# Gate stage with four ternary buffers and late down weights, and one shared down product moved to the end

## What is computed

```python
def bitlinear(x, w, norm_w):                 # gate/up: 1024 -> 2 x 2816, down: 2816 -> 1024
    xn = rms_norm(x, norm_w)
    xq = round(xn * 127 / max|xn|) per row   # integers in bf16
    wq = clip(round(w / mean|w|), -1, 1)     # ternary; one scale for the whole matrix
    return (xq @ wq.T) * scales
h = silu(gate) * up;  y = bitlinear(h, w_down, norm_down)
...
moe = sum over top-2 experts of weight * (silu(h@Wg) * (h@Wu)) @ Wd
sh  = silu(h@SWg) * (h@SWu) @ SWd            # shared expert, all tokens
x   = x + moe + sh
```

## Time and profile before

| | us |
|---|---|
| median of 3 runs | 701.76 (701.29 to 702.33) |
| the profiled execution | 699.4 |
| its span, first to last instruction | 697.6 |
| PE busy | 637.2 (91%) |
| DVE busy | 495.6 (71%) |
| ACT busy | 397.9 (57%) |
| POOL busy | 137.6 (20%) |
| mean granted PE clock | 0.983 |

### The profile page before, as it was taken

How to read it: one execution, slowest core, us unless ns; L and a number is a source line. 1 busy time by engine, 2 the same in 40 slices (tenths; PEclk the granted TensorE clock), 3 DMA queues, 4 the chain that set the end, 5 groups by cost and what they waited for, 6 DMA issues and landing times.

```text
span 697.6 us, 9765 instructions
## 1 busy us (share of the span) xinstructions
PE 637.2 (91%) x3276; PEld 476.2 (68%) x3289; DVE 495.6 (71%) x799; ACT 397.9 (57%) x524; POOL 137.6 (20%) x140
## 2 busy tenths in 40 slices
PE   4899999999998997769999999999999999999991
PEld 3778888877784342334567888787878778878771
DVE  5887778886787678888798429937465586473886
ACT  3788887887549576542673207717162673443750
POOL 2463444428401133411000400000000000000022
PEclk9999999999999999989999999999999999999996
DMA  9967776856988868606148516974738299292948
GB/s 344 371 239 307 288 287 242 333 210 220 402 343 350 344 220 337 278 0 224 49 178 305 232 70 248 363 292 168 313 132 349 95 385 390 70 382 91 352 140 321
DMA packets 30968, 179.00 MB, mean 257 GB/s; under 512 B 3808, under 2 KB 3808, under 8 KB 14688
## 3 DMA queue, kind: packets, MB, share of 16 engines
q1 hardware_dynamic: 25920, 161.39, 59.7%
q0 software_dynamic: 5024, 17.30, 6.5%
HBM read 155.62 MB, written 23.07 MB: 256 GB/s over the span
## 4 chain that ended last, share of the span: by engine, by line
PE 54%; ACT 16%; DVE 15%; issue 6%; DMA 5%; POOL 2%; DVEq 1%; ACTq 0%; POOLq 0%; SPq 0%
PE BK L288 10%; PE BK L282 10%; PE BK L283 10%; PE BK L276 6%; PE BK L1665 5%; DVE WL L945 4%; PE BK L1608 4%; ACT PR L1198 4%; ACT RA L1171 3%; ACT WH L1376 2%; PE BK L1757 2%; PE BK L1554 2%; PE BK L1539 1%; DVE HB L822 1%; DMA NG<-n_gate 1%
## 5 line engine op out<-in xcount | busy, mean ns | idle before, releaser
L282 PE MATMUL BK<-WH,ETH 128*128 128x512 f32 x272 | 107.5, 395 | 0.4
L283 PE MATMUL BK<-WL,ETH 128*128 128x512 f32 x272 | 106.0, 390 | 0.0
L945 DVE TENSOR_TENSOR WL<-RA,WH 128x2048 fp32r<-128x2048 f32 x40 | 89.1, 2286 | 9.1 <-ACT WH L1376 9.0
L1376 ACT ACTIVATE WH<-RA 128x2048 fp32r<-128x2048 f32 x40 | 73.5, 1922 | 3.1 <-PE BK L1665 3.1
L1608 PE MATMUL BK<-TG,XQ 128*128 128x512 bf16 x282 | 64.2, 386 | 11.9 <-DVE TG L796 10.2
L288 PE MATMUL BK<-WH,ETL 128*128 128x512 f32 x272 | 67.4, 390 | 0.0
L1429 ACT ACTIVATE HTH<-BK 128x256 fp32r<-128x256 f32 x34 | 12.1, 384 | 93.5 <-PE BK L1757 93.4
L282 PEld LDWEIGHTS BK<-WH,ETH 128*128 128x128 f32 x272 | 51.0, 188 | 15.9 <-DVE WL L945 4.2
L1608 PEld LDWEIGHTS BK<-TG,XQ 128*128 128x128 bf16 x288 | 28.1, 99 | 47.2 <-issue 8.9
L635 POOL DMA_INDIRECT GA<-rows,SLOT x4 | 4.7, 1176 | 277.5 <-SPq L525 276.6
L959 DVE TENSOR_TENSOR HE<-BK,SI 128x256 f32<-128x256 f32 x34 | 12.8, 420 | 64.5 <-PE BK L288 63.6
(11 more groups left out here) (245 smaller groups left out, 1368.9 us busy)
## 6 DMA issues: line engine op xcount, KB each, us to landing
RA<-wbit SPq DMA_DIRECT2D x51, 1024.0 KB, 6.4
RA<-wmoe SPq DMA_DIRECT2D x40, 1024.0 KB, 6.7
RC<-wmoe SPq DMA_DIRECT2D x20, 1024.0 KB, 7.5
RD<-wbit SPq DMA_DIRECT2D x9, 1024.0 KB, 7.8
rows<-ZERO POOLq DMA_DIRECT2D x34, 256.0 KB, 12.4
XG<-rows SPq DMA_DIRECT2D x15, 512.0 KB, 7.2
rows<-YS SPq DMA_DIRECT2D x14, 512.0 KB, 6.6
RA<-wqk SPq DMA_DIRECT2D x8, 640.0 KB, 7.4
```

Source lines behind the costliest of these rows:

```text
L282: e.matmul(dst, sh, mh, start=first and i == 0, stop=False)
L283: e.matmul(dst, sh, ml, start=False, stop=False)
L945: e.tensor_tensor(WL[m][:, q * RAW:q * RAW + RAW], RC[j][:, :], WH[m][:, q * RAW:q * RAW + RAW].bitcast(f32), ALU.subtract)\
L1376: e.activation(WH[m][:, q * RAW:q * RAW + RAW], RC[2 * m + q][:, :], ACT.Copy)\
```

## The change

- SP issues the down loads later: chunks 0 and 1 around the first gate loads, 2, 3, 8, 9, 10 spread over the later groups, 6, 7 and 4, 5 last, through the raw buffers RB[2], RB[3], RB[0], RB[1].
- The ternary weights of group c go to `gate_buffer(c)`: the two TG and the two TX in turn. DVE clamps group c+3 (not c+2) after group c.
- ACT rounds all down chunks and clamps 4 and 5 itself; DVE clamps the others. ACT's rounding of a group's two chunks stands between silus.
- The transposes and evacuation of tile 3's XQ stand earlier; PE waits for groups 2 and 3 block by block.
- The fifth and later blocks of TAIL use the SG buffers that are free; SGB goes.
- The zero writes are issued after POOL's last `norm_down`; DVE waits for them before the copy of HE.
- The down product of tiles 0 and 1 goes by thirds of k, in turn.
- Shared tile 2 keeps its transposed hidden rows (HTKH, HTKL, in H3's space) and returns before its down product; the split of expert 1's down weights comes first. In the last shared tile `kept_result` runs that product (banks 4, 5) between the up product and the transposes.
- The gathers' two halves get semaphores of their own; DVE adds routed rows of two tiles, the kept result, the routed rows of two more, and the last product's halves at the end.

```diff
 def tail_gate(c, t): return t - 2 if c == 10 and t >= 2 else t           # new
 def gate_buffer(c): return TG[c % 4] if c % 4 < 2 else TX[c % 4 - 2]     # new
 ...
# SP
-            down_load(0, 0, None)
             for n in range(4):
                 bit_load(n, 4 + n, "tern", 1 + n)
+            down_load(0, 0, None)
             ...
+            for n in range(4):
                 bit_load(n, 8 + n, "tern_a", 1 + n)
             e.wait_ge(s("zq"), NT)
             down_load(1, 1, None)
             for n in range(4):
                 bit_load(n, 12 + n, "tern", 5 + n)
-            for i in range(2, 6):
-                down_load(i, i % 2, i - 1)
...
+            for n in range(2):
+                bit_load(n, 16 + n, "tern", 9 + n)
+            down_load(2, 0, 1)
+            for n in range(2, 4):
+                bit_load(n, 16 + n, "tern", 9 + n)
+            down_load(3, 1, 2)
             for n in range(2):
                 bit_load(n, 20 + n, "tern", 13 + n)
+            down_load(8, 0, 3)
+            for n in range(2):
+                bit_load(2 + n, 2 * GC + 6 + n, "tern", 15 + n)
+            down_load(9, 1, 4)
+            for n in range(2):
+                bit_load(n, 2 * GC + 4 + n, "tern", 17 + n)
+            down_load(10, 0, 5)
# POOL, before and after the norm_down calls
-            for half in range(2 * (XT_TILES - NS)):
-                zero_rows(half)
...
+            e.memset(ZERO[:, :], 0.0).then_inc(s("zero_in"), 1)
+            e.wait_ge(s("zero_in"), 1)
+            for half in range(2 * (XT_TILES - NS)):
+                zero_rows(half)
# DVE
+            gate_weights(4)
+            group(2)
+            gate_weights(5)
+            pair_max(0)
+            group(3)
+            gate_weights(6)
+            group(4)
+            gate_weights(7)
+            down_clamp(0, RD16A)
+            pair_max(1)
...
+            group(7)
+            gate_weights(10)
+            down_clamp(3, RD16)
...
-            for t in range(1, NS):
+            for t in range(1, NS - 1):
                 shared_tile(t)
-                if t == NS - 1:
-                    split(1, 0)
-                    split(1, 1)
                 shared_result(t, t)
             split(1, 2)
+            split(1, 0, (0,))
+            e.wait_ge(s("rows"), 1)
+            hidden(NS - 1, HTKH, HTKL)
+            split(1, 0, (1,))
+            rows_lo(NS)
+            split(1, 1)
+            e.sem_inc(s("ys_d"), 1)
...
             split(NE + 1, 0)
+            result(total)
             split(NE + 1, 1)
-            result(total)
             split(NE + 1, 2)
             hidden(total)
...
+            routed(0)
+            routed(1)
+            shared_result(NS - 1, total, 4)
+            waits(e, ("ys_d", total + 2))
+            routed(NS - 1)
+            routed(NT - 1)
+            e.wait_ge(s("fin"), NT)
+            waits(e, ("y2_pe", total + 3))
             for q in range(2):
+                if q:
+                    e.wait_ge(s("sh_last"), 1)
+                v = XRES[:, NT - 1, q * 512:q * 512 + 512]
+                e.tensor_tensor(v, bank[2 + q], v, ALU.add).then_inc(s("fin"), 1)
# ACT
+            def group(c):
+                j, use = 2 * ((c + 3) % 2), (c + 3) // 2
+                gate_block(c, 0)
+                gate_block(c, 1)
+                rounded(j, use)
+                gate_block(c, 2)
+                gate_block(c, 3)
+                rounded(j + 1, use)
+            group(2)
+            group(3)
+            rounded_down(RD[:, :], s("raw_d"), 1)
+            group(4)
+            rounded_down(RD2[:, :], s("raw_e"), 1)
...
+            group(7)
+            rounded_down(RD[:, :], s("raw_d"), 3)
+            gate_block(8, 0)
+            gate_block(8, 1)
+            rounded_down(RD2[:, :], s("raw_e"), 3)
+            gate_block(8, 2)
+            gate_block(8, 3)
+            rounded_down(RB[0][:, :], in_b[0], 6)
             for n, (c, t) in enumerate(TAIL):
-                if n == 4:
-                    rounded_last(2)
-                    rounded_last(3)
...
+                if n == 1:
+                    rounded_down(RB[1][:, :], in_b[1], 6)
+                elif n == 3:
+                    sign_down(4, 0, 7)
+                elif n == 4:
+                    rounded_down(RB[2][:, :], in_b[2], 5)
+                elif n == 6:
+                    rounded_down(RB[3][:, :], in_b[3], 5)
...
+            hidden_t(0)
+            rounded_down(RD[:, :], s("raw_d"), 4)
+            sign_down(5, 1, 8)
+            hidden_t(1)
# PE
+            for c in (2, 3):
+                e.wait_ge(s("tern_a"), 2 * c - 2)
+                for t in range(NT):
+                    e.wait_ge(s("h"), 9 + HEAD.index((c - 2, t)))
+                    gate_block(gate_buffer(c), 4 * (c % 2) + t, t)
+            for c in range(4, 9):
+                gate_group(c, c % 2, gate_buffer(c), "tern", 2 * c - 2)
...
             hidden_t(0)
+            e.wait_ge(s("h"), 8 + 36 + 4)
+            e.wait_ge(s("ternd"), 4)
+            down_group(0, 0)
+            hidden_t(1)
+            e.wait_ge(s("h"), 8 + 44)
+            down_group(1, 0)
+            e.wait_ge(s("tern_a"), 6)
+            e.wait_ge(s("ternd"), 8)
+            down_group(0, 1)
+            down_group(1, 1)
...
+            def kept_result():
+                waits(e, (free_c[4], NE + 2), (free_c[5], NE + 2))
+                for q in range(2):
+                    for h in range(2):
+                        highs(e, bank[4 + q], y_high(h, q, HTKH), h == 0)
+                    m = lows(e, bank[4 + q], y_low(q, HTKL))
+                m.then_inc(s("y2_pe"), 1)
```

More of the change, by code:

```diff
@@ L1304, in _ @@
             sign(3, 3)
[L1305 removed]
             e.preload_act_table(ACT.Silu)
+            rows_out(3)
             def head_block(n):
@@ L1318, in head_block @@
                     .then_inc(s("silu"), 1)
-            for n in range(3):
-                head_block(n)
-            rows_out(3)
-            for n in range(3, 6):
+            for n in range(7):
                 head_block(n)
             rounded(0, 2)
+            head_block(7)
             rounded(1, 2)
-            for n in range(6, 8):
-                head_block(n)
-            rounded(2, 2)
-            rounded(3, 2)
-            rounded_down(0)
-            def gate_block(n, t, bank_):
-                waits(e, ("g_pe", n + 2), ("h", n + 5))
-                e.activation(SG[t][:, :], bank_[:, 0:GW], ACT.Silu, scale=col(9)[:, t:t + 1]).then_inc(s("silu"), 1)
@@ L1350, in _, with gate_block, group @@
-            for j in (0, 1):
-                rounded(j, 5)
-            gate_group(8, 0)
-            e.wait_ge(s("ternd"), 9)
+            def gate_block(c, t):
+                n = 4 * c + t
+                waits(e, ("g_pe", n + 2), ("h", n + 5))
+                e.activation(SG[t][:, :], bank[4 * (c % 2) + t][:, 0:GW], ACT.Silu, scale=col(9)[:, t:t + 1])\
+                    .then_inc(s("silu"), 1)
+            def group(c):
+                j, use = 2 * ((c + 3) % 2), (c + 3) // 2
[5 more added lines that the diff above has]
+                rounded(j + 1, use)
@@ L1438, in _ @@
             e.activation(WT[:, 1, :], E1[:, :, :].rearrange("p a b -> p (a b)"), ACT.Exp).then_inc(s("e1"), 1)
-            for t in range(1, NS):
+            for t in range(1, NS - 1):
                 hidden(t)
+            split(1, NS - 1, (2,))
+            e.wait_ge(s("rows"), 1)
+            hidden(NS - 1, True, HTKH)
             e.sem_inc(s("ys_a"), NS)
-            split(1, NS)
+            split(1, NS, (1,))
             e.wait_ge(s("ys_d"), NS)
@@ new lines, in _ @@
+            e.wait_ge(s("tern_a"), 6)
+            e.wait_ge(s("ternd"), 8)
+            down_group(0, 1)
+            down_group(1, 1)
+            e.wait_ge(s("ternd"), 9)
+            down_group(0, 2)
+            hidden_t(2)
+            down_group(1, 2)
+            for t in (2, 3):
+                e.wait_ge(s("hqt"), 3 * t + 3)
+                e.wait_ge(s("x3"), t - 1)
+                for q in range(2):
+                    down_part(t, q, 0, KB).then_inc(s("d_pe"), 1)
+                    if t == 2 and q == 0:
+                        hidden_t(3)
@@ L1758, in tile @@
                     m.then_inc(s("ht2_pe"), 1)
-                if more:
-                    rows_t(t + 1, 1, rows)
+                if not more:
+                    last_result(t)
+                    return
+                rows_t(t + 1, 1, rows)
+                if isinstance(t, int) and t == NS - 1:
+                    e.sem_inc(s("y2_pe"), 1)
+                    return
                 left = [("ys_a", t + 1), ("ys_d", t + 1)] if not isinstance(gi, int) or gi else [("ys_d", t)]
-                waits(e, ("ht_hi", t * 2 + 1), *left, (free_c[4], gi + 1), (free_c[5], gi + 1))
@@ L1773, in tile, with down_at, y_high @@
                 e.wait_ge(s("ht_lo"), t * 2 + 2)
                 for q in range(2):
```

(24 more changed lines are left out.)

244 lines of the change are left out of this document (102 added, 142 removed).

## The result

| | before | after |
|---|---|---|
| median, 4 runs each on one chip | 701.52 us (700.08 to 702.33) | 681.67 us (681.32 to 683.29) |
| the profiled execution | 699.4 | 681.58 |
| its span | 697.6 | 680.0 |
| mean granted PE clock | 0.983 | 0.987 |

Ratio 0.972, 95% interval 0.9699 to 0.9741: faster. Two more batches measured the changed kernel at 683.08 (0.9753) and 683.13 (0.9743), 5 runs each, so 682 to 683 is the fairer figure. The medians before and after are 19.9, 17.1 and 17.8 us apart in the three batches. Forecast: 681.5, range 676 to 691.

The account below looks back on a forecast made before the run. PE was taken as held up in the gate stage, mostly by late ternary weights, and the end as set by gathers and DVE. Terms -1.7 - 15.3 + 0.9 - 5.2 + 1.0 = -20.3 gave 681.5 us, range 676 to 691.

Parts of the forecast that it names:

- Zero rows: Before the gate stage: with the zero writes issued later, NG lands sooner and PE's wait at ZQ goes, -1.7 us.
- Gate stage: PE runs the gate blocks without waiting for ternary weights; the HQ transposes start near 296.0, not 311.25: -15.3 us.
- From there the queue never empties: Gate stage: after down 1's clamp at 250.3 the load queue stays full, so down 9 lands at 277.8.
- bounds 0 to +3: Gate stage: DVE clamps stretched beside POOL in five places, 0 to +3 us in all, taken as 0.
- Down product: Down product of the first tiles by thirds: PE waits for HQT, 46.6 us instead of 45.7, +0.9, bounds 0 and +3.8.
- Moved product: Third shared tile's down product moved to the end: tile 3's transposes come sooner, -5.2 us, bounds -5.4 and -2.
- End: After the up product: gathers land sooner but DVE starts later with a longer list, +1.0 us, bounds -3 and +3.
- A: Rival, gate stage: the loads, not ACT, set the pace; four laps pay 1.8 us each, 689 us; chance 0.17.
- B: Rival, gate stage: late raw weights hold silus, hidden blocks and the clamps that free buffers; slower, 704 us; chance 0.04.
- C: Rival, experts: the moved product brings nothing; the middle gives back 5 us, the end pays 1, 686.5 us; chance 0.08.
- D: Rival, gate stage: PE still waits for clamps, so only -9.5 us comes, 692 us; chance 0.06.

Follow-up runs that it names:

- the narrow products: The changed kernel with each of POOL's norm products in the gate stage covering 16 columns, the rest left out: 663.66 us, ratio 0.9478 to the kernel before.
- the clamps moved ahead: The changed kernel with DVE's clamps of down 1 and 3 in front of gate clamps 8 and 10: 681.12 us, ratio 0.9719 to the kernel before.
- the execution with both changes: The changed kernel with down clamps 1 and 3 ahead and the last tile's transposes before the kept result: 681.30 us, ratio 0.9723 to the kernel before.
- the six executions: Six profiled executions with the changed kernel's gate stage; first gate matmul to first HQ transposes took 88.7 us in the mean.
- the experiment: The changed gate stage with the experts and end of the kernel before, kept product undone: 686.93 us, ratio 0.9807 to the kernel before.
- the run with late clamps: The changed kernel with gate clamps 4 to 10 a group later, first three down clamps moving too: 714.70 us, ratio 1.0205 to the kernel before.

## Why the prediction was right, and where its steps were not

1. **Zero rows** (-1.7). First ZQ transposes at 184.82 without a wait, against 187.10: -2.3. DVE's weight scales came at 174.08 (forecast 174.5), NG in 4.0 us. The writes took longer to issue than in the earlier trace rows, and held nobody:

```profile
308.17 21.89 POOL L572 DMA_DIRECT2D rows<-ZERO  x34 [0.32 <-POOL ZERO L627]
```

2. **Gate stage** (-15.3). Transposes of HQ at 297.13, against 311.25: -14.1 with item 1 in it, -11.8 without. Short by 3.5. PE's part was right: no waits but 0.8, clock 1.00, through at 286 (288.1 less item 1 is 286.4). The step that failed is "From there the queue never empties". It stood on a down clamp that follows its gate clamps at once, and on a stretch of DVE's clamps beside POOL taken as 0 since "such a clamp delays a load whose queue is full anyway". The trace has the DMA share at 0.48 at that very clamp. ACT waited 6.7 us, not 3.9, and began down 9's rounding 71.1 us behind the first gate matmul, where the forecast had 277.8 - 210.6 = 67.2. That is 3.9 late and so the whole miss. The two stretches of 4 us at 135 and 320 GB/s are worth 2.7 and 1.0 us of a queue that moves 430, an estimate, and come to as much. The stretch of the clamps was in the earlier trace rows with bounds 0 to +3; the narrow products put it at 1.8, and the clamps moved ahead, which get round the same stretch, at 2.0 (1.3 in the execution with both changes). With the clamps ahead the same two stretches move 375 and 418 GB/s, and down 9's rounding still begins at 69.0; what holds back that rest was not tried. The Trainium skill (SBUF — State Buffer, "SBUF: two separate sides") has the port pair of DVE and GpSimd as an exclusive lock that the first takes for its whole instruction. The pair of clamps at 2.91 beside POOL and 1.30 without its long products agrees; I had used that rule for POOL's issues alone and not for DVE's clamps.
3. **Down product** (+0.9): 45.92 against 45.74: +0.2, and +0.6 in the mean of the six executions. PE's wait for HQT was there, 0.91. Within its bounds.
4. **Moved product** (-5.2): from tile 1's transposes to tile 3's 32.69 us against 437.36 - 399.62 = 37.74: -5.05; by the experiment -4.97. The lower clock that the new wait brought in two of twelve executions (+1.5) had no term. PE waited 1.41 for ETH and not again, 1.1 and 0.3 had been forecast.
5. **End** (+1.0): from the last up product to the last instruction +0.75, DVE without a gap, as told. The end of the kernel before took 21.95 and 23.01 us in the two executions that have it, so neither the size nor the sign of this term is shown.

The profiled spans differ by 17.6, the sum had 20.3: the gate stage's 3.5 too much, against it 0.6 that item 1 brought beyond its term and 0.7 that item 3 cost less, and small ones. That the median fell on the forecast is partly luck: the profiled execution before was 2.4 us quicker than its median, the one after was not, and that offset, added to the forecast, covered the miss. In the profiled execution's own terms the forecast was 679.1, and it took 681.58. Against the later batches (683.1) the forecast is 1.6 low.

Of the rivals, A's sign (loads late, by latency and issue) was in part true, at 3.5 us and not 7.5; B's ring exists and is dear, but half a group's delay does not close it and a whole group's, with the down clamps behind it, does; C and D fell, by the run without the kept product and by PE's 0.8 us of waits.

## What to carry to other kernels

- On an engine that works in order, what a late load costs is what stands behind its consumer. Putting that consumer behind the work that needs nothing from it brought 4.0 us here, twice what an earlier load did.
- A stage fed by a ring of buffers (clamp, issue, landing, rounding, clamp) has slack or it has none: half a group later cost 0.2 us, a group later with the down clamps behind it over 31. Work out a lap with the latency of one load before pricing a delay as a single step.
- The instruction that releases the next load goes in front of its neighbours, above all where these are stretched.
- A gain that ends in front of a dense stretch of PE is partly given back where PE enters that stretch sooner but at a low granted clock and ahead of its operands: of 5.3 us gained ahead of the down product, 2.6 went in it.

## What was not expected of the hardware

- DVE's int16 to bf16 clamps of 128x2048 take 0.65 us, and 1.3 to 1.45 in the mean of a pair beside POOL's 128x512 products; whichever kind of clamp comes first is hit (a down clamp moved to that place took 1.23 instead of 0.68).
- POOL's issues were slower beside DVE work with two operands in SBUF: 2.11 and 1.87 us for a gather beside the WL split, 0.93 behind it, and up to 1.72 when DVE's sums were moved beside them. The plain zero writes took 21.89 / 34 = 0.64 us each beside DVE's work in the down product, against 0.54. Only the sums were moved by an experiment; for the split and the zero writes the cause is argued from what ran beside them.
- A short wait of PE can cost as much again. In ten of the twelve profiled executions with the moved product the matmuls behind the wait for ETH took their usual 0.39 to 0.40 us, with the granted clock at 1.00; in two they took up to 0.63, with 0.57 over the 4 us behind the wait, and the stretch was 1.5 us longer. The length of the wait alone does not tell them apart: 1.45 and 1.46 us in those two, 1.41 to 1.58 in the others.
- A load of 1 MB with the queue empty took 4.8 us from its issue to ACT's start in the run with late clamps, as before the change (4.7), and a ring of single loads pays it in every lap.
